# Attention context stored unscaled with its sums, inverses by memory once per batch, product on GpSimd in the last stage

## What is computed

```python
scores = (scores + rel_q + rel_k) / jnp.sqrt(jnp.asarray(D, scores.dtype))
probs = jax.nn.softmax(scores, axis=-1)
ctx = jnp.einsum('bhqk,bhkd->bhqd', probs, v)
ctx = ctx.transpose(0, 2, 1, 3).reshape(B, S, E)
h = ctx @ Wo + bo + hidden_states
```

## Time and profile before

| | us |
|---|---|
| median of 3 runs (2950.71 to 2954.8) | 2954.4 |
| the profiled execution | 2954.29 |
| its span | 2952.5 |
| PE busy in the span | 2521.0 |
| DVE busy | 2049.5 |
| POOL busy | 1896.4 |
| ACT busy | 1623.3 |

### The profile page before, as it was taken

How to read it: one execution, slowest core, us unless ns; L and a number is a source line. 1 busy time by engine, 2 the same in 40 slices (tenths; PEclk the granted TensorE clock), 3 DMA queues, 4 the chain that set the end, 5 groups by cost and what they waited for, 6 DMA issues and landing times. The chain is left out here.

```text
span 2952.5 us, 53450 instructions
## 1 busy us (share of the span) xinstructions
PE 2521.0 (85%) x19084; PEld 1750.5 (59%) x19084; DVE 2049.5 (69%) x5771; ACT 1623.3 (55%) x2069; POOL 1896.4 (64%) x1535
## 2 busy tenths in 40 slices
PE   4877748887887887779999999999999589999998
PEld 2554537776776776646666666666666345555553
DVE  4655526776777677657777777777777478888884
ACT  1443535665655566457878787878788312222222
POOL 2333246466575655478888888888888545566664
PEclk7998957877777777689999999999999799999999
DMA  3577589999999999999999999999999412222210
GB/s 114 185 244 252 172 267 403 395 385 376 390 407 368 400 392 373 386 291 338 309 307 305 303 310 305 301 323 306 307 303 301 143 67 75 82 76 75 75 47 24
DMA packets 301960, 773.59 MB, mean 262 GB/s; under 512 B 37608, under 2 KB 104496, under 8 KB 258048
## 3 DMA queue, kind: packets, MB, share of 16 engines
q1 hardware_dynamic: 276880, 659.84, 65.1%
q10 hardware_dynamic: 18160, 87.26, 9.2%
q0 software_dynamic: 6656, 23.07, 2.2%
HBM read 417.39 MB, written 352.63 MB: 261 GB/s over the span
## 5 line engine op out<-in xcount | busy, mean ns | idle before, releaser
L903 POOL TENSOR_SCALAR t_neg<-t_neg,t_low 128x512 f32<-128x512 f32 x512 | 794.9, 1567 | 120.1 <-DVE t_low L1104 115.8
L1104 DVE CUSTOM_DVE_ANT_1 t_neg<-t_ps,t_r 128x512 f32<-128x512 f32 x1024 | 667.6, 686 | 250.8 <-issue 245.9
L1166 ACT ACTIVATE t_eT<-t_pt 128x1024 f32<-128x1024 f32 x512 | 524.4, 1024 | 212.2 <-PE t_pt L1023 211.5
L1023 PE MATMUL t_pt<-t_ident,t_neg 128*128 128x128 f32 x4096 | 617.3, 273 | 5.2 <-POOL t_neg L903 4.7
L1023 PEld LDWEIGHTS t_pt<-t_ident,t_neg 128*128 128x128 f32 x4096 | 517.0, 142 | 83.1 <-POOL t_neg L903 6.3
L1488 PE MATMUL e_pX<-e_we,e_h2T 128*128 128x512 f32 x1024 | 455.8, 596 | 14.3 <-DVE e_even L1696 14.3
L1011 PE MATMUL t_ps<-t_kb,t_qa 96*128 96x512 bf16 x1024 | 399.2, 390 | 60.7 <-DVE t_low L1104 36.9
L787 DVE TENSOR_TENSOR d_r<-d_pq,d_r 128x1024 f32<-128x1024 f32 x256 | 298.7, 1218 | 149.9 <-ACT d_r L758 123.3
L1156 ACT ACTIVATE t_neg<-t_neg,t_low 128x512 f32<-128x512 f32 x512 | 369.0, 721 | 45.3 <-DVE t_low L1104 45.3
L787 DVE TENSOR_TENSOR ad_nat<-d_pq,ad_nat 128x1024 f32<-128x1024 f32 x256 | 299.3, 1218 | 129.7 <-ACT ad_nat L758 92.1
L659 POOL COPY d_q<-d_q 32x2048 f32<-32x2048 f32 x104 | 196.3, 1888 | 279.3 <-DMA d_q<-q_by_place_scratch 275.8
(11 more groups left out here) (154 smaller groups left out, 3261.5 us busy)
## 6 DMA issues: line engine op xcount, KB each, us to landing
t_r<-r_scratch SPq DMA_DIRECT2D x1024, 256.0 KB, 6.9
r_scratch<-d_r SPq DMA_DIRECT2D x128, 1024.0 KB, 10.1
r_scratch<-ad_nat SPq DMA_DIRECT2D x128, 1024.0 KB, 7.9
d_q<-q_by_place_scratch ACTq DMA_DIRECT2D x52, 256.0 KB, 5.5
ad_nat<-q_by_place_scratch ACTq DMA_DIRECT2D x52, 256.0 KB, 6.3
q_rows_scratch<-a_part SPq DMA_DIRECT2D x16, 768.0 KB, 4.7
k_rows_scratch<-a_part SPq DMA_DIRECT2D x16, 768.0 KB, 3.7
q_by_place_scratch<-ad_nat SPq DMA_DIRECT2D x6, 2048.0 KB, 11.5
```

The source lines that it names most:

```text
L903: nc.gpsimd.tensor_scalar(neg[:, j % RING, t, :], neg[:, j % RING, t, :], low[:, j % RING, t:t + 1], None, ALU.subtract).then_inc(pool_sub, 1)
L1023: last = nc.tensor.transpose(p_t[t // 2][:, t % 2, c, :], neg[:, j % RING, t, c * P:(c + 1) * P], ident[:])
L1104: nc.vector.tensor_tensor_reduce(out=neg[:, j % RING, t, :].rearrange("p (c r) -> p c r", r=TB), in0=p_s[t % 2][:].rearrange("p (c r) -> p ...
L1166: nc.scalar.activation(to, p_t[half][:], ACT.Exp, scale=(1.0 if half else -1.0)).then_inc(exped, 1)
```

## The change

In attention the context and its sums are stored as they come out of ScalarE's emptying: `store` waits for that, writes the 16 rows of each of four heads as before and one more DMA with the four rows of sums, and stands three groups behind (LAG) instead of four. Once per batch SyncE loads the 16 x 512 sums back as 128 partitions of 64 (`load_sums`), VectorE inverts them in one instruction (`invert`, at head 14, tile 3 of the following batch) and SyncE stores the inverses (`store_inv`). TensorE's two sets of transposes, GpSimd's widening and VectorE's product are gone from this stage.

In experts SyncE loads for each batch, behind its context, 16 rows of inverses, each to the 16 partitions of its head, and GpSimd multiplies the context by them (`scale`) before it makes hb and xb of the same batch; TensorE's projection waits for that. The sums of the last batch are inverted at the start of this stage.

```diff
@@ -804,7 +804,7 @@
-def attention(nc, rows_d, v_d, r_d, cT_d, nb=NB):
+def attention(nc, rows_d, v_d, r_d, cT_d, sums_d, inv_d, nb=NB):
@@ -841,13 +841,12 @@
 cs = sb("t_cs", [P, CS, S])
-inv = sb("t_inv", [P, TT, GH])
-wide = sb("t_wide", [P, GT, CT])
+sums = sb("t_sums", [P, H * S // P])
+inv = sb("t_inv", [P, H * S // P])
 tiny = sb("t_tiny", [P, 8])
...
 p_c = ps("t_pc", [P, S])
-p_i = ps("t_pi", [P, S])
@@ -868,13 +867,12 @@
 emptied = sem("t_emptied")
-summed = sem("t_summed")
+sums_loaded = sem("t_sums_loaded")
 inverted = sem("t_inverted")
-widened = sem("t_widened")
-spread = sem("t_spread")
-scaled = sem("t_scaled")
+inv_stored = sem("t_inv_stored")
 ctx_stored = [sem(f"t_ctx_stored{i}") for i in range(CS)]
-STORE = 16 * GH
+STORE = 16 * (GH + 1)
+LAG = 3
@@ -910,21 +908,12 @@
-        def widen(G):
-            pool.wait_ge(inverted, G + 1)
-            later(pool, spread, G)
-            nc.gpsimd.tensor_copy(wide[:], inv[:].rearrange("p t j -> p (t j)").unsqueeze(2)
-                                  .to_broadcast([P, GT, CT])).then_inc(widened, 1)
         def head(step, j):
...
                     subtract(n, j, t)
-            if j % GH == 1 and (not fixed or 2 * GH <= n):
-                widen(2 * step + j // GH - 2)
             if j % GH == 1 and (not fixed or n < NH):
@@ -968,12 +957,27 @@
-            sp.wait_ge(scaled, BG * b + k + 1)
             G = BG * b + k
+            sp.wait_ge(emptied, G + 1)
             for j in range(GH):
...
                              ).then_inc(ctx_stored[G % CS], 16)
+            sp.dma_start(sums_d[b, GH * k:GH * (k + 1), :], cs[D:P:CT, G % CS, :]).then_inc(ctx_stored[G % CS], 16)
+        def load_sums(b):
+            for i in range(CS):
+                sp.wait_ge(ctx_stored[i], STORE * ((BG * b + BG - 1 - i) // CS + 1))
+            later(sp, inverted, b)
+            sp.dma_start(sums[:], sums_d[b].rearrange("h s -> (h s)").rearrange("(p x) -> p x", p=P)
+                         ).then_inc(sums_loaded, 16)
+        def store_inv(b):
+            sp.wait_ge(inverted, b + 1)
+            sp.dma_start(inv_d[b].rearrange("h s -> (h s)").rearrange("(p x) -> p x", p=P), inv[:]
+                         ).then_inc(inv_stored, 16)
@@ -982,8 +986,12 @@
                     load_v(b, k)
-                if j % GH == 1 and BG * b + k >= 4:
-                    store(b + (k - 4) // BG, (k - 4) % BG)
+                if j % GH == 1 and BG * b + k >= LAG:
+                    store(b + (k - LAG) // BG, (k - LAG) % BG)
+                if j == 5 and b >= 2:
+                    store_inv(b - 2)
+                if j == 13 and b >= 1:
+                    load_sums(b - 1)
@@ -994,8 +1002,10 @@
                 batch(g, last, u)
-        for k in range(BG - 4, BG):
+        for k in range(BG - LAG, BG):
             store(nb - 1, k)
+        store_inv(nb - 2)
+        sp.wait_ge(inv_stored, 16 * (nb - 1))
@@ -1037,22 +1047,6 @@
-        def sums(G):
-            pe.wait_ge(emptied, G + 1)
-            later(pe, scaled, G)
-            for t in range(TT):
-                last = nc.tensor.transpose(p_i[:, t * P:(t + 1) * P], cs[:, G % CS, t * P:(t + 1) * P], ident[:])
-            last.then_inc(summed, 1)
-        def widen(G):
-            pe.wait_ge(widened, G + 1)
-            for t in range(TT):
-                last = nc.tensor.transpose(p_i[:, t * P:(t + 1) * P],
-                                           wide[:, t * GH:(t + 1) * GH, :].rearrange("p j w -> p (j w)"), ident[:])
-            last.then_inc(spread, 1)
         def head(step, j):
@@ -1067,11 +1061,6 @@
                         weigh(G, (k // GT - 1) % 2, (k % GT - 6) // 4 + c)
-                G = 2 * step + k // GT - 2
-                if k % GT == 4 and (not fixed or 0 <= G < NGR):
-                    sums(G)
-                if k % GT == 9 and (not fixed or 0 <= G < NGR):
-                    widen(G)
@@ -1107,16 +1096,11 @@
-        def invert(G):
-            dve.wait_ge(summed, G + 1)
-            sums = p_i[:].rearrange("p (t j w) -> p t j w", j=GH, w=CT)[:, :, :, D]
-            nc.vector.reciprocal(inv[:], sums).then_inc(inverted, 1)
-        def scale(G):
-            dve.wait_ge(spread, G + 1)
-            nc.vector.tensor_tensor(cs[:, G % CS, :], cs[:, G % CS, :], p_i[:], ALU.mult).then_inc(scaled, 1)
+        def invert(b):
+            dve.wait_ge(sums_loaded, 16 * (b + 1))
+            later(dve, inv_stored, 16 * b)
+            nc.vector.reciprocal(inv[:], sums[:]).then_inc(inverted, 1)
@@ -1138,11 +1122,8 @@
                     copy_q(b, m)
-                G = 2 * step + k // GT - 2
-                if k % GT == 5 and (not fixed or 0 <= G < NGR):
-                    invert(G)
-                if k % GT == 11 and (not fixed or 0 <= G < NGR):
-                    scale(G)
+                if t == 3 and n % H == H - 2 and H <= n < NH:
+                    invert(n // H - 1)
@@ -1217,7 +1198,7 @@
-def experts(nc, ins, mod_d, h_d, cT_d, out, nb=NB):
+def experts(nc, ins, mod_d, h_d, cT_d, sums_d, inv_d, out, nb=NB):
@@ -1251,6 +1232,9 @@
 cT = sb("e_cT", [P, 2, KC, S])
+ib = sb("e_inv_rows", [P, 2, KC, S])
+last_sums = sb("e_sums", [P, H * S // P])
+last_inv = sb("e_last_inv", [P, H * S // P])
 hb = sb("e_hb", [P, 2, TT, E])
@@ -1296,6 +1280,10 @@
 ctx_loaded = [sem(f"e_ctx_loaded{u}") for u in range(2)]
+sums_loaded = sem("e_sums_loaded")
+inverted = sem("e_inverted")
+inv_stored = sem("e_inv_stored")
+ctx_scaled = sem("e_ctx_scaled")
 in_loaded = [sem(f"e_in_loaded{u}") for u in range(2)]
@@ -1337,6 +1325,12 @@
             sp.dma_start(cT[:, u], cT_d[b].rearrange("(k p) l -> p k l", p=P)).then_inc(ctx_loaded[u], 16)
+            if b == nb - 1:
+                sp.wait_ge(inv_stored, 16)
+            for row in range(H):
+                k, part = divmod(row, P // D)
+                sp.dma_start(ib[part * D:(part + 1) * D, u, k, :], inv_d[b, row].partition_broadcast(D)
+                             ).then_inc(ctx_loaded[u], 16)
@@ -1355,8 +1349,14 @@
         load(1)
+        sp.dma_start(last_sums[:], sums_d[nb - 1].rearrange("h s -> (h s)").rearrange("(p x) -> p x", p=P)
+                     ).then_inc(sums_loaded, 16)
         for b in range(2, nb):
             load(b)
+            if b == 2:
+                sp.wait_ge(inverted, 1)
+                sp.dma_start(inv_d[nb - 1].rearrange("h s -> (h s)").rearrange("(p x) -> p x", p=P), last_inv[:]
+                             ).then_inc(inv_stored, 16)
@@ -1382,6 +1382,12 @@
             last.then_inc(sums_done, 1)
+        def scale(b):
+            u = b % 2
+            pool.wait_ge(ctx_loaded[u], 16 * (H + 1) * (b // 2 + 1))
+            nc.gpsimd.tensor_tensor(cT[:, u], cT[:, u], ib[:, u], ALU.mult).then_inc(ctx_scaled, 1)
@@ -1411,12 +1417,15 @@
             pool.dma_start(gb[:, u], mod_d[u, GB_, :].partition_broadcast(P)).then_inc(gb_loaded[u], 16)
+        scale(0)
         sums(0)
+        scale(1)
         sums(1)
...
             if b + 2 < nb:
+                scale(b + 2)
                 sums(b + 2)
@@ -1431,7 +1440,7 @@
-            pe.wait_ge(ctx_loaded[u], 16 * (b // 2 + 1))
+            pe.wait_ge(ctx_scaled, b + 1)
             later(pe, bias_out, b - 1)
@@ -1704,6 +1713,8 @@
         x1_norm(0)
+        dve.wait_ge(sums_loaded, 16)
+        nc.vector.reciprocal(last_inv[:], last_sums[:]).then_inc(inverted, 1)
         dve.wait_ge(w_loaded, NW)
@@ -1734,6 +1745,8 @@
     cT_d = scratch("ctx_scratch", [NB, E, S])
+    sums_d = scratch("sums_scratch", [NB, H, S])
+    inv_d = scratch("inv_scratch", [NB, H, S])
     r_d = [scratch(f"r{g}_scratch", [NT, P, RPITCH]) for g in range(NG)]
@@ -1749,8 +1762,8 @@
 distances(nc, tab_d, n_d, r_d, nat, stored)
-    attention(nc, rows_d, v_d, r_d, cT_d)
-    experts(nc, ins, mod_d, h_d, cT_d, out)
+    attention(nc, rows_d, v_d, r_d, cT_d, sums_d, inv_d)
+    experts(nc, ins, mod_d, h_d, cT_d, sums_d, inv_d, out)
...
 def kernel(**inputs):
```

## The result

The changed kernel is slower. Its median is 2988.5 us (four runs, 2980.5 to 2996.1) against 2953.1 for the kernel before, timed beside it: a ratio of 1.012, 95% interval 1.0092 to 1.0148. The forecast was 2934. Against the span of before, 2952.5, it is 41.8 us longer: 1.3 ahead of attention, 3.2 in attention (1066.5 us instead of 1063.3) and 37.3 in the last stage (659.9 instead of 622.6). The forecast for these two was -40.6 and +20.

The account below looks back on a forecast made before the run. TensorE, 97% busy, and what holds it up were taken to set attention. The terms -45 + 7 - 2.6 + 5 + 15 = -20.6 us on 2954.3 us gave 2934 us, range 2914 to 2957.

Parts of the forecast that it names:

- rival 3: Attention: R loads cannot go faster than today, so attention gains nothing; 2972 us, chance 0.10.
- SyncE's 242 us of waiting for slots: Attention: argument against DMA being the limit, SyncE waiting 242 of 900 us for a free R slot.
- 354 GB/s over 20 us of the same stage: Attention: argument against DMA being the limit, a higher rate seen over 20 us than the stage's 304 GB/s.
- TensorE's sets: Attention: removing two transpose sets saves 0.73 us per group, 45 us over 62 groups.
- Rival 1: Attention: only TensorE's own time counts, ScalarE's exp comes early enough; 13 us more gain, 2921 us, chance 0.17.
- Reciprocal: Attention, VectorE: 15 reciprocals of 128x64, estimated 0.57 us each, make TensorE wait 0.47 us each, 7 us given back.
- Attention as a whole, with the drain: Attention and its closing stores: 45 us saved, 7 given back and 2.6 saved between the stages.
- "Nothing" for the sums' and inverses' traffic: DMA: two small DMAs per batch and the sums per group are nothing beside 1 MB of R per head.
- Start of the last stage: Sixteen row loads ahead of the modulation rows delay the start by 5 us, bounds 3.2 and 7.7.
- Last stage per batch: GpSimd's product ahead of its sums makes VectorE start 1.1 us later; 15 us over 14 batches.
- the "0.2" for the finishes of GpSimd: Last stage: GpSimd's fourth-tile finish, pushed over VectorE's short normalisation products, costs 0.2 us per batch.
- Rival 2: Last stage: GpSimd's scale is slowed by VectorE's two-input products; 28 us instead of 15, 2947 us, chance 0.13.

Follow-up runs that it names:

- Experiment 17: Kernel before the change, with only half of R laid out and fetched in 4 KB pieces: 2973.2 us, ratio 1.0055 to the kernel before.
- experiment 16: Changed attention with half of R in 4 KB pieces, last stage of the kernel before, division left out: 2942.0 us, ratio 0.9946 to the kernel before.
- experiment 6: Changed attention without storing and loading sums, reciprocal or storing inverses, with the last stage of before: ratio 0.9953 to the kernel before.
- experiment 12: Changed kernel with GpSimd's product left out and the row loads kept: ratio 0.9969 to the kernel before.
- experiment 8: Changed kernel with GpSimd's product moved after the first tile's finish and batch 0's rows issued from ScalarE's queue: ratio 0.999 to the kernel before.

## Why the prediction was wrong

The step that failed is the rejection of rival 3: "DMA shows a share of 1.02 and 304 GB/s over the stage", set aside because of "SyncE's 242 us of waiting for slots" and "354 GB/s over 20 us of the same stage". The rival's number, 318 needed and under 311 to be had, was right: 305 came (311 in the shortest execution of the same attention), 319 to 320 is taken where it can be had. Its 2972 us and the 17 us by which the last stage is dearer than forecast make 2989, against 2988.5 measured. Both arguments against it were wrong readings.

- SyncE's wait for slots doesn't say that DMA has room. A queue that issues ahead into a ring waits for slots whenever the ring is full, and it is full as soon as supply covers demand, by however little. 242 us of 900 were not 27% of spare rate: 4% more demand used them up. Experiment 17 shows what more room looks like in the same view, 409.6 us of 700.
- The 354 GB/s stand at the same moment in the changed kernel too, with its share of 1.06, and that kernel comes to 305 in the mean. Over 1500 to 2200 us of the kernel before, slices of 17.5 us go from 278 to 353 GB/s, every one with DMA busy at 90% or more: 20 us are too short to tell what the stage can get.

Point by point, where R is out of the way (experiment 16):

- TensorE's sets, 62 x 0.73 = 45 us. Halves of 7.67 and 8.00 us make a group of 15.67 instead of 16.28, 0.61 us: 38 us. Forecast 15.55. Rival 1 is refuted by the turn that waits for ScalarE's exp.
- Reciprocal, 7 us. 0.55 us each (0.57 estimated); a half with one takes 8.04 instead of 7.67, so 15 x 0.37 = 5.5 us.
- Attention as a whole, with the drain: -40.6 forecast, -37.6 measured in experiment 16. In the profiled execution of the changed kernel +3.2, 41 us lost to R; the shortest of the six has -17.1, 21 us lost. By the medians some 30 are lost.
- "Nothing" for the sums' and inverses' traffic: some 6 us by the medians where R isn't met, not clear of noise (experiment 6).
- Start of the last stage, +5: the first addition is 3.3 us late, the stage 4.0 with the loads alone (experiment 12).
- Last stage per batch, 1.1 us: it is 2.16 in the batch shown. The product took the 2.35 us assumed for it, and the sums were late by 0.8 as worked out. What was mis-sized is the "0.2" for the finishes of GpSimd that slide over VectorE: 1.36 us. Over fourteen batches the term is some 15 us short. Rival 2 had nearly the right size, 28 us for 30, by a wrong mechanism and so by luck: the product was never slowed (2337 to 2347 ns in all sixteen). It was VectorE that was held. The rule of the Trainium skill quoted ahead ("SBUF — State Buffer", Who interferes with whom) would have said so for `e_first`, `e_an` and `e_x`, with two inputs in SBUF, had it been laid over every instruction that moved and not over the product alone. `e_var` has one input and isn't covered by the rule as quoted; the trace shows it held all the same, 0.72 us instead of 0.17. What the sum doesn't hold at all is the clock: six stretches at half clock in the last stage, behind TensorE's longer waits.

Of the last stage's 37.3 us, 5.5 are the later first projection, 31.0 the fifteen intervals from it to the last batch's (14 x 2.16 would be 30.2), and 0.7 what comes behind.

## What to carry to other kernels

Where DMA's busy share stands at 1 over a stage, every microsecond that a change takes from an engine there has to be multiplied out in GB/s first, and set against a rate that the same pieces have reached over a long stretch. Neither the share nor a queue that waits for free slots tells the room: the share was 1.01 with transfers to spare (experiment 17) and 1.03 without. Ask whether the pieces can be made longer over all partitions, and what the stage that writes them pays. Work moved to an engine with margin is to be laid out with everything that it pushes, and against what the other engines run at those new times, TensorE's granted clock behind a longer wait included; the same product in a real gap (experiment 8) was free.

## What was not expected of the hardware

- The rate of loads from memory to SBUF at full DMA share depends on the piece per partition: the changed attention with pieces of 2 KB got 305 to 311 GB/s at a share of 1.02 to 1.04 in this mixture, with half of R at 4 KB 317 to 319 at 1.01 to 1.02, with all of it at 8 KB 320 at 0.97. At 319 and 320 attention asked for no more, so these are not their limits.
- Splitting the same loads by partitions, 0 to 31 and 32 to 127, cost 22% of the rate at full share (239 GB/s), and 233 with mixed pieces.
- A VectorE instruction of 128x32, 0.66 us alone, took 2.28 us when GpSimd had begun a product of 2.35 us 0.12 us before it. In the long batches it is the conversion before it (`e_atf`, one input) that is held: 1.68 to 1.70 us instead of 0.36.
- At or just behind six of eight waits of TensorE of 2.8 to 3.0 us in the last stage the granted clock stood at 0.50 for 3.4 us or more; behind the other two, and behind waits of 0.97 and 1.7 us there, it didn't.
